# Conditioning moved from GpSimd to ScalarE and VectorE, heads alternated on TensorE

## The reference, cut to what matters

```python
ek = exp(min(k, 30)); ekv = ek * v
a = a * decay + ekv_t;  b = b * decay + ek_t        # scanned forward (nf, df) and backward (nb, db)
euk = exp(min(u + k, 30))
num = nf + nb - ekv + euk * v
den = df + db - ek + euk
base = sigmoid(r) * (num / maximum(den, 1e-08)) * (0.8 + 0.2 * tf)
```

```python
h = h * dA_t + (dt_t * x_t) * B_t;  y = C_t . h     # done as masked matmuls over 128x128 tiles
```

## Time and profile before

| what | us |
|---|---|
| median of 3 timed runs (1410.77 to 1413.26) | 1410.94 |
| profiled execution, its own time | 1404.55 |
| profiled execution, span from the first to the last instruction | 1402.8 |
| busy: TensorE / VectorE / ScalarE / GpSimd | 1195.4 / 850.6 / 581.1 / 568.0 |

### The profile page before, as it was taken

How to read it: one execution, slowest core, us unless ns; L and a number is a source line. 1 busy time by engine, 2 the same in 40 slices (tenths; PEclk the granted TensorE clock), 3 DMA queues, 4 the chain that set the end, 5 groups by cost and what they waited for, 6 DMA issues and landing times. The chain is left out here.

```text
span 1402.8 us, 16347 instructions
## 1 busy us (share of the span) xinstructions
PE 1195.4 (85%) x4614; PEld 644.4 (46%) x4614; DVE 850.6 (61%) x1244; ACT 581.1 (41%) x1710; POOL 568.0 (40%) x531
## 2 busy tenths in 40 slices
PE   0059999699995999999968989888898888988998
PEld 0024554355543444444434646443783437844443
DVE  7979996699964752364248749369541695414232
ACT  2025555365542322232226646567571675701110
POOL 5574876248763310020026749357540475400000
PEclk9999999999997999999989999989899898997999
DMA  6000000000034000000030000030000000000000
GB/s 260 0 22 1 1 1 1 1 0 0 0 124 162 0 0 0 0 0 0 34 150 1 1 0 0 17 126 1 1 2 1 1 1 0 1 8 0 0 0 30
DMA packets 5485, 33.28 MB, mean 24 GB/s; under 512 B 528, under 2 KB 1936, under 8 KB 3536
## 3 DMA queue, kind: packets, MB, share of 16 engines
q1 hardware_dynamic: 5424, 32.61, 6.0%
HBM read 31.56 MB, written 1.05 MB: 23 GB/s over the span
## 5 line engine op out<-in xcount | busy, mean ns | idle before, releaser
L806 POOL TENSOR_TENSOR decays<-decays,scores 128x768 f32<-128x768 f32 x64 | 122.6, 1920 | 117.5 <-ACT decays L742 117.2
L575 PE MATMUL pg<-h,weights 128*128 (+1 forms) x136 | 67.5, 621 | 78.0 <-PEq L356 76.7
L1991 POOL TENSOR_TENSOR f_pair<-m,weights 128x256 f32<-128x256 f32 x80 | 91.0, 1156 | 95.4 <-DVE m L2012 94.3
L1094 PE MATMUL ph<-h,weights 128*128 x256 | 115.8, 597 | 0.0
L1399 POOL TENSOR_TENSOR prob_latent<-prob_latent,inverse_latent 128x128 f32<-128x128 f32 (+1 forms) x128 | 81.5, 660 | 70.1 <-DVE inverse_latent L1389 69.7
L742 ACT ACTIVATE decays<-pcum,neg_cum 128x256 f32<-128x256 f32 (+1 forms) x256 | 86.3, 426 | 9.9 <-PE pcum L628 9.6
L1239 DVE TENSOR_TENSOR mid<-up,ph 128x512 f32<-128x512 f32 x44 | 30.2, 687 | 98.5 <-ACT up L1151 98.5
L1399 POOL TENSOR_TENSOR prob_gqa<-prob_gqa,inverse_gqa 128x128 f32<-128x128 f32 (+1 forms) x128 | 62.1, 506 | 58.3 <-DVE inverse_gqa L1389 56.5
L879 DVE SCALAR_TENSOR_TENSOR conv<-px,pp,conv 128x510 f32<-128x510 f32 (+2 forms) x102 | 75.9, 744 | 15.9 <-ACT conv L714 13.5
L1151 ACT ACTIVATE up<-ph 128x512 f32<-128x512 f32 x44 | 26.3, 597 | 140.5 <-PE ph L1094 140.5
L575 PE MATMUL px<-h,weights 128*128 x136 | 70.5, 643 | 14.0 <-DVE conv L879 14.0
(11 more groups left out here) (326 smaller groups left out, 2981.7 us busy)
## 6 DMA issues: line engine op xcount, KB each, us to landing
weights<-in_w_mixer SPq DMA_DIRECT2D x2, 2048.0 KB, 18.4
weights<-in_w_moe SPq DMA_DIRECT2D x2, 1536.0 KB, 8.0
moe_rest<-in_w_moe SPq DMA_DIRECT2D x2, 1536.0 KB, 13.5
weights<-in_w_gqa SPq DMA_DIRECT2D x1, 3072.0 KB, 10.2
weights<-in_w_gqa SPq DMA_DIRECT2D x1, 2048.0 KB, 14.6
weights<-in_w_moe SPq DMA_DIRECT2D x1, 1920.0 KB, 8.7
weights<-in_w_mixer SPq DMA_DIRECT2D x1, 1536.0 KB, 12.6
weights<-in_w_moe SPq DMA_DIRECT2D x1, 1152.0 KB, 12.0
```

The costliest lines, as they stand in the source:

```text
L575: op = nc.tensor.matmul(out[0:m, :], w[:, col + k * m:col + (k + 1) * m], net.h[:, ds(i * PAIR + k * TOK, TOK)], start=(k == 0), stop=(k = ...
L806: nc.gpsimd.tensor_tensor(decays[:, head % 4], decays[:, head % 4], scores[:], ALU.mult).then_inc(decay_scaled, 1)
L1094: op = nc.tensor.matmul(out[:], wt[:, n * D + k * P:n * D + (k + 1) * P], net.h[:, ds(i * PAIR + k * TOK, TOK)], start=(k == 0), stop=(k = ...
L1991: op = nc.gpsimd.tensor_tensor(out[:, :, s, :], src[:, :, 1 - s, :], sin[:, None, s, :].to_broadcast([P, 4, HALF]), ALU.mult)
```

## The change

The conditioning no longer uses GpSimd. Spreading the decay and copying `e` go to ScalarE; the products with `f`, the subtraction and the two additions of the numerator go to VectorE, in two halves each, so its list grows from 26 to 36 entries. The copy of `f` is gone. In the first stage alone, ScalarE inverts the denominator as exp(-ln), with one more table load, and VectorE does the denominator first and then the numerator. In the other stages VectorE keeps its reciprocal. In `mix` the two heads alternate, and one wait covers both.

```diff
+    def scalar_operands(self, pair, turn):
+        nc.scalar.wait_ge(self.factor_made, turn)
         for kt in range(KT):
...
+            for b in range(BB):
+                at = (kt * BB + b) * SEG
+                col = net.dcol[:, ds((self.c * KT + kt) * BATCH + pair * BB + b, 1)]
+                nc.scalar.activation(net.decay[:, at + 1:at + SEG],
+                                     net.ones[:, 0:1].to_broadcast([P, SEQ]), ACT.Copy,
+                                     scale=col).then_inc(self.decay_spread, 1)
+        nc.scalar.activation(net.e_pair[:], net.e[:, ds(pair * UNIT, UNIT)], ACT.Copy) \
+            .then_inc(self.e_copied, 1)
...
+    def scalar_invert(self, turn):
+        nc.scalar.wait_ge(self.bounded, turn + 1)
+        nc.scalar.activation(net.den[:], net.den[:], ACT.Ln).then_inc(self.inverted, 1)
+        nc.scalar.wait_ge(self.inverted, 2 * turn + 1)
+        nc.scalar.activation(net.den[:], net.den[:], ACT.Exp, scale=-1.0) \
+            .then_inc(self.inverted, 1)
...
         stages = [
-            add_u,
-            scan(net.den, net.e, 2), scan(net.num, net.ev_pair, 3),
-            scan(net.num_b, net.ev_pair, 3, True), scan(net.den_b, net.e_pair, 4, True),
-            combine(net.den, net.den_b), add_own, bound,
+            add_u, e_times_f,
+            scan(net.den, net.e, den_done), scan(net.num, net.ev_pair, num_done), own,
+            scan(net.num_b, net.ev_pair, num_b_done, True),
+            scan(net.den_b, net.e_pair, den_b_done, True),
+            own_times_f,
+            combine(net.num, net.num_b, num_done, num_b_done),
+            combine(net.den, net.den_b, den_done, den_b_done),
+            combine(net.num, net.ev_pair, num_done, ev_done),
+            combine(net.den, net.euk, den_done, own_done), bound,
         ]
...
         @block.scalar
...
-            unit.scalar(0, 0)
+            unit.scalar_operands(0, 0)
+            unit.scalar_exp(0)
             tanh_h()
-            unit.scalar(1, 1)
+            nc.scalar.preload_act_table_set("natural_log_exp_and_others")
+            unit.scalar_invert(0)
+            unit.scalar_operands(1, 1)
+            unit.scalar_exp(1)
+            unit.scalar_invert(1)
...
-                for hh in range(TILE_HEADS):
-                    head = s * TILE_HEADS + hh
-                    pe.wait_ge(decay_scaled, i * HEADS + head + 1)
-                    rows = slice(hh * HEAD, (hh + 1) * HEAD)
-                    for b in range(BB):
-                        for r in range(ST):
-                            cols = slice(0, SEQ) if r == 0 else slice(SEQ, TRI)
+                pe.wait_ge(decay_scaled, i * HEADS + (s + 1) * TILE_HEADS)
+                for b in range(BB):
+                    for r in range(ST):
+                        cols = slice(0, SEQ) if r == 0 else slice(SEQ, TRI)
+                        for hh in range(TILE_HEADS):
+                            head = s * TILE_HEADS + hh
+                            rows = slice(hh * HEAD, (hh + 1) * HEAD)
...
                 begin_conv(i, 0)
                 begin_conv(i, 1)
+                unit.scalar_operands(i, i + PAIRS)
...
                     if s == 3:
-                        unit.scalar(i, i + PAIRS)
+                        unit.scalar_exp(i + PAIRS)
...
             with nc.gpsimd.Fori(0, PAIRS) as i:
-                unit.pool_operands(i, i + PAIRS)
-                numerator = list(unit.pool_numerator(i + PAIRS))
...
-                    if s in (5, 8, 9, 10):
-                        numerator.pop(0)()
...
+                    if m == 1 and unit:
+                        unit.scalar_operands(i, i + turn0)
...
+                    if u == 1:
+                        unit.scalar_operands(i, i + 3 * PAIRS)
```

More of the change, by code:

```diff
@@ L249, in columns @@
             return slice(k * n, (k + 1) * n), ds(pair * UNIT + k * n, n)
[L252 to L259, removed]
+        num_done, den_done, ev_done, own_done = ([None] * KT for _ in range(4))
         def add_u(k):
@@ L267, in add_u, with e_times_f, scan @@
                 op.then_inc(self.u_ready, 1)
-        def scan(out, x, operands, reverse=False):
+        def e_times_f(k):
+            here, both = columns(k)
+            ev_done[k] = link.mark(v.tensor_tensor(net.ev_pair[:, here], net.e[:, both],
+                                                   net.f[:, both], ALU.mult))
+        def scan(out, x, done, reverse=False):
             def step(k):
                 here, both = columns(k)
-                v.wait_ge(self.operand_ready, 4 * turn + operands)
+                v.wait_ge(self.decay_spread, KT * BB * turn + (k + 1) * BB)
+                if x is net.ev_pair:
+                    v.wait_ge(*ev_done[k])
+                if x is net.e_pair:
+                    v.wait_ge(self.e_copied, turn + 1)
@@ L284, in scan, with own @@
-            return step
-        def combine(a, b):
+                done[k] = link.mark(v.tensor_tensor_scan(
+                    out[:, here][:, order], net.decay[:, here][:, order],
+                    data[:, order] if reverse else data, 0.0, ALU.mult, ALU.add))
+            return step
+        def own(k):
+            here, both = columns(k)
+            v.wait_ge(self.euk_ready, turn + 1)
+            own_done[k] = link.mark(v.tensor_tensor(net.euk[:, here], net.euk[:, here],
+                                                    net.e[:, both], ALU.subtract))
@@ L288, in step, with own_times_f, combine @@
+        def own_times_f(k):
+            here, both = columns(k)
+            v.wait_ge(*own_done[k])
+            v.wait_ge(*num_b_done[k])
+            ev_done[k] = link.mark(v.tensor_tensor(net.ev_pair[:, here], net.euk[:, here],
+                                                   net.f[:, both], ALU.mult))
+        def combine(a, b, a_done, b_done):
             def step(k):
                 here, _ = columns(k)
-                after(k)
-                on(k, v.tensor_tensor(a[:, here], a[:, here], b[:, here], ALU.add))
@@ L303, in invert @@
+            op = v.tensor_scalar(net.den[:, here], net.den[:, here], 1e-8, None, ALU.max)
+            if self.bounded is None:
+                den_done[k] = link.mark(op)
+            elif k == KT - 1:
+                op.then_inc(self.bounded, 1)
         def invert(part):
@@ L305, in invert @@
             if part % (INVERT_PARTS // KT) == 0:
-                after(part * KT // INVERT_PARTS)
+                v.wait_ge(*den_done[part * KT // INVERT_PARTS])
             op = v.reciprocal(net.den[:, cols], net.den[:, cols])
```

117 lines of the change are left out of this document (37 added, 80 removed).

## The result

The changed kernel takes 1378.22 us (median of 4 runs, 1377.15 to 1379.72), the kernel before 1410.86 beside it: a ratio of 0.9767, 95% interval 0.975 to 0.9784. That is 32.6 us less; the forecast was 35.5. The total is close, but two of its terms missed by 6 and by 9 us in opposite directions. Split at TensorE's first and last matmul of each part, the profiled spans show it.

The account below looks back on a forecast made before the run. No single engine bounds the whole: VectorE bounds the first stage, TensorE and VectorE are level in the mixer. First stage 22.2, mixer 9.3, pair starts 2.0, latent attention 1.0 and 1.0 make 35.5 off 1410.94: 1375 us, range 1367 to 1382.

Parts of the forecast that it names:

- First stage, 22.2: Stage before the mixer: VectorE's list without GpSimd and with the hidden inversion ends earlier, 22.2 us gained after 0.5 for spreads.
- The timed median is 6.4 above that execution, so I take the same 35.5 from 1410.94: Whole kernel: the 35.5 us worked out on the profiled execution of 1404.55 is taken off the timed median, giving 1375.
- The mix, 2.15 to 1.45: Mixer, TensorE: alternating heads overlap throughout, so a mix takes 1.45 us instead of 2.15, 0.70 less a step.
- Rivals 3 and 4: Mixer's mix: alternating brings nothing, stays 2.15, 1386 us (chance 0.06); or heads run one behind the other, 2.71, 1404 (0.04).
- rival 5: Mixer: added steps land on VectorE's path at the disturbed 2.31 us each, so the kernel gets slower, 1431 us; chance 0.04.
- The twelve full steps, 1.85 a pair: Mixer steps 3 to 14: VectorE keeps most of TensorE's saving, 105.7 us against 107.55, 1.85 less for a pair.
- rival 1: Mixer: VectorE's collisions with GpSimd fall away, TensorE sets the twelve steps at 8.35 us, 11 more gained, 1364; chance 0.16.
- The last four steps, 2.8 gained a pair: End of a mixer pair: four mixes on the path gain 0.70 us each, 2.8, and the new reciprocals fit into VectorE's wait.
- Pair starts, 2.0: Mixer pair starts: VectorE no longer waits behind GpSimd's conditioning, 2.0 us gained for both pairs; ScalarE's copies may cost 0 to 5.
- First expert stage 0, latent attention 2.0: Expert stage: TensorE never stops, nothing shows. Latent attention: 1.0 us from the opening step, 1.0 from the units.
- Rival 2: Latent attention becomes VectorE's: the added entries and 1.0 us of ScalarE show in both pairs, 14 us, 1390; chance 0.10.
- The stages behind them, 0: Groups behind the latent attention are not touched, so no gain or loss was counted there.

Follow-up runs that it names:

- the second profile: The kernel before, unchanged, profiled once more: 1408.66 us, span 1406.9, first mixer matmul at 83.3 us against 76.7 in the profile the prediction used.
- both_first: The changed kernel with both conditioning steps of a mixer step taken ahead of the gating of x: 1355.44 us, ratio 0.961.
- square_later: The changed kernel with one added wait: GpSimd adds the square of step 17's tile only after VectorE's next `g`: 1372.52 us, ratio 0.9753.
- longer_prologue: The kernel before with 40 one-column memsets at the very start of VectorE's program, loop body unchanged: 1408.62 us, in one run.
- wide_first: both_first with products, additions and bound of the mixer's conditioning as single instructions of 1028 columns instead of two of 514: 1354.37 us, ratio 0.9623.
- combined: wide_first with 1028-column instructions in the first stage too, and GpSimd's waits of square_later in steps 16 and 17: 1346.79 us, ratio 0.9564.
- heads_only: The kernel before with the alternation of the heads in the mix alone: 1401.90 us, ratio 0.9942.

## Why the prediction was right, and where it was not

- **First stage, 22.2: right** against its profile, which gives 21.7. The durations without GpSimd, the spreads and the hidden inversion all held.
- **"The timed median is 6.4 above that execution, so I take the same 35.5 from 1410.94": wrong.** The 6.4 was read as a constant offset. It is the meeting of VectorE and GpSimd in the first stage, and the change removes it: against the second profile the first stage gives 28.3. This added 6 us that no term of the sum had.
- **The mix, 2.15 to 1.45: right** (1.46, with eight matmuls in each half). Rivals 3 and 4 fall with it, rival 5 with the total. The Trainium skill's rule cited there (TensorE: Matmul & The Clock Gate, Part 3 (The mechanism)) is not what this trace shows either: weight loads are busy 0.53 us in the same 0.70 us as eight matmuls of the two heads.
- **The twelve full steps, 1.85 a pair: right by one measure only.** From mix to mix they take 108.5 instead of 110.6 us. From convolution to convolution, which is how the prediction added them up, they take 107.46 (375.73 - 268.27) instead of 107.55, not 105.7: the first takes 9.92 us, and three of them take 9.2. The mix only follows the convolution more closely at the end (2.04 us behind it instead of 4.07). That VectorE beside GpSimd sets them, and not TensorE, both_first shows: rival 1's mechanism, brought about on purpose, gives 8.0 us a pair where that rival had 5.5. In the changed kernel itself the collisions stay, so rival 1 falls.
- **The last four steps, 2.8 gained a pair: wrong, and the largest miss.** They lost 2.0 in the first pair and 1.7 in the second. The reciprocals did fit in, as forecast; the term left out what else these steps meet. In the second pair the shorter mix moved `g` to the moment when GpSimd begins a sum of squares (1.1 us), and TensorE's next matmuls ran at the lower clock (1.3 more). In the first pair the collision cost 0.2, and the lower clock came twice. And one of the steps takes 7.06 even at full clock, where it took 6.58 before: TensorE waits in it for ScalarE's decays. So in square_later, where the clock never falls here, these steps gain 0.9 a pair from mix to mix, not 2.8.
- **Pair starts, 2.0: half right.** The first pair starts 2.3 earlier (39.3 us from the first matmul to the first mix instead of 41.6). The second starts 0.7 later: VectorE's loop now takes 2.84 us for its way back, where it took 0.36. In the second pair ScalarE's spreads cost nothing: they end at 239.5, and VectorE's input for the softplus comes at 241.4. In the first they hold the softplus up by 0.4 us (66.1 to 66.5).
- **First expert stage 0, latent attention 2.0:** together 3.0, and a pair of the latent attention takes 71.1 us instead of 72.8. Rival 2 falls.
- **The stages behind them, 0:** 1.7 lost against the one profile and 3.3 against the other, with unchanged code and a different granted clock.

So the mixer gave 2.2 of the forecast 11.3, and the first stage 6 more than forecast; that the sum came out right by 3 us is luck, since these errors nearly cancel. The parts don't add up to 32.6 either: against the second profile they give 29.2, chiefly because that execution lies 2.2 us under its kernel's median and the profile after 1.5 over its own. Where these 3.4 us lie no run shows.

## What to carry to other kernels

A median that lies apart from the profiled execution is a quantity to explain before it is subtracted from: take a second profile, and ask whether the change removes what differs. When a step gets shorter, look at what its successor now meets on the engine that was not in the way before. Two engines that hold each other up can be parted by moving an instruction a few places, or by one wait: here that was worth more (23 us) than the faster matmuls were before it was done (2).

## What the runs showed of the hardware

- **VectorE and GpSimd on additions and products in SBUF.** The one that comes second waits until the other's instruction is done: 0.69 becomes 2.33 (products), 1.81 (`g`), 2.83 (additions beside steps of 2.7 us). Reciprocals beside GpSimd's additions lose nothing (6.66 for the eight, with or without GpSimd beside them; 2.35 for a GpSimd step). Where one is already waiting, either may be let in next: the same order of starts ended in two ways in two executions, 6 us apart. The Trainium skill, SBUF — State Buffer (SBUF: two separate sides), says that whichever starts first gets the shared port pair for the whole instruction. The single meetings agree; that GpSimd, already waiting, is passed by three more additions in one execution and by none in the other, it does not say.
- **A loop's way back on VectorE: 0.34 to 0.36 us or 2.84 to 3.01.** It was short where up to 434 records of VectorE lay between the program's start and the branch, long from 455 on; the length of the body alone (337 in longer_prologue as in the kernel before) does not decide, and wide_first (long) and combined (short) have the same body of 348 records. ScalarE's own loop takes 2.4 to 2.7 us in every profile, with 360 to 384 records ahead of its branch, so the count is VectorE's alone. The Trainium skill, Runtime: NRT & Kernel Launch (Instruction fetch mechanics), says that a taken branch out of the two pages of instructions that are held has to fetch its target. That the place of the loop decides agrees with it; that the time goes into a fetch no run shows, and the exact size can't be read off the runs, since not all instructions ahead of the loop are in the records.
- **The granted clock moves unchanged code.** From the grouped-query attention to the end the same instructions took 478.9 to 484.2 us in the profiles, as much as many edits are worth. And behind the same 2.78 us of idle time it stayed at 1.00 in the one pair of heads_only and was 0.50 in the other.
